# Upsampling matmuls on eight array tiles of 32x64 instead of two of 64x128, with the orders of TensorE, ScalarE and VectorE rewritten

## The chip, the cores and the metric

The kernel runs on one NeuronCore of one Trainium2 chip. The metric is the device time of one execution in microseconds, the median of several runs. The core has TensorE (PE, matmuls; its weight loads are listed as PEld), VectorE (DVE), ScalarE (ACT), GpSimd (POOL) and SyncE (SP, which here issues DMAs). Each runs its own instruction stream; they meet at semaphores only.

## What is computed

x is f32 of shape (8, 512, 128, 128). Layer 0 downsamples it with a 3x3 stride-2 convolution (256 channels, 64x64), clusters the channels, derives a gate per channel, and adds the gated and bilinearly doubled map to x. Layer 1 adds a bias, upsamples rows and columns by 2 with a 12-tap filter, applies leaky ReLU with a gain of sqrt 2, and downsamples by 2 with the 12-tap filter:

```python
def _L0(sx, w_down, w_conv, w_up):
    x = conv(sx, w_down, stride=2)             # (8, 256, 64, 64)
    ...                                        # clusters, mixture fit, gate
    pre_up = gate[:, :, None, None] * x + x
    up = jnp.repeat(pre_up, 2, axis=1) * w_up[None, :, None, None]
    return _bilinear_up_x2(up) + sx

def _L1(input, bias, up_filter, down_filter):
    out = input + bias[None, :, None, None]
    out = _sep_upfirdn(out, up_filter * 2, 2, 1, UP_PAD)     # 128x128 -> 256x256
    out = leaky_relu(out, 0.2) * sqrt(2)
    return _sep_upfirdn(out, down_filter, 1, 2, DOWN_PAD)    # 256x256 -> 128x128
```

## The kernel before

The program has five stages: `convolution`, `clusters`, `cluster_means`, `mixture` and, from about 1665 us on, `resample`. The change lies in `resample` alone.

`resample` handles the 4096 images (128x128) four at a time: a pair u is two units e of two images i, and there are PAIRS = 1024 of them. Each engine has a function `slot(u, r, m)` that issues its work of slot u; `schedule` (L863) unrolls the first and last slots and loops over the others, STEP = 4 slots to a turn, with the slot number r*4+m in registers. `cnt` gives a semaphore's target for a slot; where it depends on r, a register instruction computes it. `has(u, lag)` says whether a stage that runs `lag` slots behind has work in slot u, `after(u, n)` whether a wait is needed yet.

A pair passes these stages, in different slots:

- SP: `load_low` (L892, every second slot, two buffers), `load_img` (L904), `store` (L914).
- Every second slot (a group of two pairs): TensorE doubles the rows of the small map (L1044, `b1_acc`, in bank 6), ACT copies it (L1100, `low_v`), POOL doubles the columns (L956 to L962, `lift`). POOL adds the bias to `img` (L947).
- DVE: `x_sum` = lift*coef + img, four instructions (L1135), for pair u+1 in slot u.
- TensorE, first upsampling of pair u: `x_sum` is the stationary operand, the banded filter matrix `up_t` the moving one. The band lets the contraction over 128 rows be cut in two halves of 64; `upper` (L980) uses 133 columns of `up_t`, `lower` (L985) the other 133, on the upper and lower 64 rows of the array. Two row tiles may not write one bank at a time, so the first half of the work gives image i=0 to `upper` and i=1 to `lower`, and the second half the other way round, with the waits `u1_half`/`u2_half` on TensorE's own semaphores between. Results: `u1_acc` (banks 0, 1).
- DVE: copies both banks to `up1` (L1144).
- TensorE, second upsampling of pair u-1: the same from `up1` into `u2_acc` (banks 2 to 5).
- ACT: `slope` (L1091), a scaled copy `slope_t` of each of the four banks. DVE: `leaky` = max(GAIN*bank, slope_t) (L1152), four instructions.
- TensorE: `first_down` of pair u-2 from `leaky` into banks 6 and 7, 32 matmuls; ACT copies them (L1117, `dn1`). Then d2 of pair u-3 from `dn1` into bank 0, 16 matmuls; ACT copies it (L1108, `res`), and SP stores it. Both use L991, tiles of 128x64, 67 columns.

Order in a slot now: TensorE does first and second upsampling (first half), the group's L1044 product, their second halves, d2, `first_down`. DVE does x_sum, copies, leaky. ACT does low_v, two slopes, res, two slopes, dn1. An f32 matmul appears in the trace as two LDWEIGHTS and two MATMUL records.

Of the kernel before, what the change touches and what calls it, by code (L numbers as in the profile page):

```python
# [13 lines left out]
P = 128  # L14
# [26 lines left out]
UP_REACH = 2 * HALF + 5  # L41
# [46 lines left out]
def build(nc, x, w_down, w_conv, w_up, bias, up_filter, down_filter, consts, out):  # L88
    at = constants()[1]
    ctx = ExitStack()  # L90
    with ctx:
# [713 lines left out]
        def resample():  # L805
            with ExitStack() as own:
# [8 lines left out]
                low = [sb(f"low{i}", [HO, LOWS, WO]) for i in range(2)]  # L815
# [12 lines left out]
                low_loaded = [sem(f"low_loaded{i}") for i in range(2)]  # L828
# [7 lines left out]
                u1_half = sem("u1_half")  # L836
                u1_mm = sem("u1_mm")
                u1_out = sem("u1_out")
                u2_half = sem("u2_half")
                u2_mm = sem("u2_mm")  # L840
# [12 lines left out]
                d2_acc = bank[0]  # L853
                b1_acc = bank[6][:, 0:LOWS * WO]
# [6 lines left out]
                STEP = 4  # L861
                LOOP0, LOOP1 = STEP, PAIRS - STEP

                def schedule(eng, slot):

                    for u in range(FIRST, LOOP0):
                        slot(u, 0, u)
                    with eng.Fori(LOOP0 // STEP, LOOP1 // STEP) as r:
                        for m in range(STEP):
# [12 lines left out]
                def cnt(u, r, m, k, per=1, of=1):  # L882
# [3 lines left out]
                    return r * (STEP // of * per) + (m + k) // of * per  # L886
# [4 lines left out]
                def _(sp):  # L891
                    def load_low(u, r, m):  # L892

                        p = (m // 2) % 2
                        g = cnt(u, r, m, 4, per=2)
                        done = cnt(u, r, m, 2, of=2)
                        if u is None:
                            g, done = sp.snap(g), sp.snap(done)
                        if after(u, 0):
                            sp.wait_ge(b1_mm, done)  # L900
                        sp.dma_start(low[p][:], lows[:, bass.ds(g, LOWS), :] if u is None else lows[:, g:g + LOWS, :]).then_inc(low_loaded[p], 16)
# [20 lines left out]
                    def slot(u, r, m):  # L922
                        if m % 2 == 0 and has(u, -4):
                            load_low(u, r, m)
                        if has(u, -2):
                            load_img(u, r, m)
# [47 lines left out]
                def _(pe):  # L974

                    pe.wait_ge(ready, 2 + 2 * FT)

                    def upper(acc, src, first):

                        return pe.matmul(acc[:, 0:UP_REACH], src, up_t[0:HALF, 0:UP_REACH],  # L980
                                         start=first, stop=False, skip_group_check=True)

                    def lower(acc, src, first):

                        return pe.matmul(acc[:, UH - UP_REACH:UH], src, up_t[HALF:P, UH - UP_REACH:UH],  # L985
                                         start=first, stop=False, skip_group_check=True)
# [9 lines left out]
                    def first_up(e, i, p, half, first):  # L996
                        tile = (upper, lower)[half]
                        return tile(u1_acc[i][:, e * UH:(e + 1) * UH], x_sum[p][HALF * half:HALF * (half + 1), e, i, :], first)

                    def second_up(e, i, p, half, k, first):  # L1000
                        tile = (upper, lower)[half]
                        return tile(u2_acc[e][i][:, k * UW:(k + 1) * UW],
                                    up1[p][HALF * half:HALF * (half + 1), i, e, k * P:(k + 1) * P], first)
# [10 lines left out]
                    def slot(u, r, m):  # L1014
                        group = m % 2 == 0 and has(u, -2)
                        p = m % 2
                        if has(u, 0):
                            pe.wait_ge(x_summed, cnt(u, r, m, 1))
                            if after(u, 1):
# [166 lines left out]
```

## Time and profile before

| | us |
|---|---|
| median of 3 runs | 7928.65 (7927.54 to 7929.11) |
| profiled execution | 7925.67 |
| its span, first to last instruction | 7923.9 |
| busy: PE, DVE, ACT, POOL | 7411.7, 6318.9, 4073.0, 2543.3 |
| mean granted TensorE clock over the span | 0.969 |

The page gives busy times over the whole span, while 6.3 of its 7.9 ms are one stage, `resample`. So the page says which groups there are, the stretches say how busy each engine is in that stage, and the timeline of one slot shows who waits for whom. Records of PE overlap one another: a group's busy time is not the count times the mean. The start of a record is measured, its end modelled.

### The profile page before, as it was taken

Reading aid. Unit: us, or ns where it says so; the run is one execution under the profiler, and the core shown is the slowest. Engines: PE = TensorE matmul, PEld = TensorE weight load, DVE = VectorE, ACT = ScalarE, POOL = GpSimd, SP = SyncE. Lnnn points to the kernel's source line nnn. Section 1 sums busy time; section 2 is a strip of 40 time slices with the busy share of each in tenths; the row PEclk is TensorE's granted clock in tenths of the full one; section 3 lists DMA queues with packets and bytes.
Section 4 is the critical chain, followed back from the end, with each engine's and each line's share of the span. In section 5 each row is a group of like instructions: output and inputs, shape, how many; then the busy total and the mean of one; then the engine's idle time right before and its main releaser. Section 6 shows DMA issues by size and latency. Waiting matters only on the chain.

```text
span 7923.9 us, 374577 instructions
## 1 busy us (share of the span) xinstructions
PE 7411.7 (94%) x151493; PEld 6562.6 (83%) x151493; DVE 6318.9 (80%) x12643; ACT 4073.0 (51%) x8046; POOL 2543.3 (32%) x3076
## 2 busy tenths in 40 slices
PE   7999966069999999999999999999999999999999
PEld 3444441059999999999999999999999999999999
DVE  8999942878888888888888888888888888888887
ACT  0000002346666666666666666666666666666666
POOL 0000000024444444444444444444444444444443
PEclk9999978579999999999999999999999999999999
DMA  7777714013333333333333333333333333333333
GB/s 307 313 306 316 310 58 180 0 55 91 92 90 92 90 93 90 93 90 92 91 92 90 92 91 92 91 91 92 91 92 91 92 90 93 90 92 91 93 90 87
DMA packets 1253328, 925.41 MB, mean 117 GB/s; under 512 B 175312, under 2 KB 1224912, under 8 KB 1234384
## 3 DMA queue, kind: packets, MB, share of 16 engines
q1 hardware_dynamic: 1243920, 890.10, 34.7%
q10 hardware_dynamic: 9344, 34.61, 1.6%
q8 instruction: 22, 0.36, 0.0%
q14 instruction: 42, 0.34, 0.0%
HBM read 621.50 MB, written 303.04 MB: 117 GB/s over the span
## 4 chain that ended last, share of the span: by engine, by line
PE 79%; DVE 0%; POOL 0%; DMA 0%; ACT 0%; issue 0%; POOLq 0%; DVEq 0%
PE bank L991 38%; PE bank L980 30%; PE bank L985 9%; PE bank L1044 2%; DVE x_sum L1135 0%; DMA img<-in_x 0%; DMA low<-conv_dram 0%; ACT slope_t L1091 0%; DVE leaky L1152 0%; POOL low_f L959 0%; POOL img L947 0%; ACT dn L1117 0%; POOL low_d L956 0%; POOL lift L962 0%; ACT low_v L1100 0%
## 5 line engine op out<-in xcount | busy, mean ns | idle before, releaser
L1152 DVE SCALAR_TENSOR_TENSOR leaky<-bank,slope_t 128x512 f32<-128x512 f32 x4096 | 2637.2, 685 | 575.6 <-ACT slope_t L1091 511.2
L1091 ACT ACTIVATE slope_t<-bank 128x512 f32<-128x512 f32 x4096 | 2219.8, 597 | 1697.8 <-PE bank L985 1697.8
L980 PE MATMUL bank<-up_t,up 64*128 64x133 f32 x16384 | 2186.2, 273 | 1.4 <-DVE leaky L1152 1.2
L985 PE MATMUL bank<-up_t,up 64*128 64x133 f32 x16384 | 2186.3, 273 | 0.0
L991 PE MATMUL bank<-down_t,leaky 128*64 128x67 f32 x65536 | 2086.2, 222 | 0.0
L980 PEld LDWEIGHTS bank<-up_t,up 64*128 64x128 f32 x16384 | 2009.0, 187 | 2.4 <-DVE leaky L1152 1.0
L985 PEld LDWEIGHTS bank<-up_t,up 64*128 64x128 f32 x16384 | 2006.3, 187 | 0.0
L991 PEld LDWEIGHTS bank<-down_t,leaky 128*64 128x64 f32 x65536 | 1999.0, 137 | 0.1
L1144 DVE COPY up<-bank 128x512 f32<-128x512 f32 x2048 | 1318.7, 685 | 626.6 <-PE bank L985 626.6
L956 POOL TENSOR_TENSOR low_d<-low_v 128x252 f32<-128x252 f32 x512 | 310.9, 607 | 4023.6 <-ACT low_v L1100 4023.6
L985 PE MATMUL bank<-up_t,x_sum 64*128 64x133 f32 x8192 | 1521.0, 299 | 0.0
L947 POOL TENSOR_TENSOR img<-img,bias_all 128x512 f32<-128x512 f32 x1024 | 1064.4, 1040 | 1288.0 <-DMA img<-in_x 1288.0
L980 PE MATMUL bank<-up_t,x_sum 64*128 64x133 f32 x8192 | 1363.6, 286 | 8.5 <-DVE x_sum L1135 6.5
L980 PEld LDWEIGHTS bank<-up_t,x_sum 64*128 64x128 f32 x8192 | 1112.9, 187 | 99.1 <-DVE x_sum L1135 7.3
L991 PE MATMUL bank<-down_t,dn 128*64 128x67 f32 x32768 | 1182.4, 225 | 2.1 <-ACT dn L1117 1.5
L1135 DVE SCALAR_TENSOR_TENSOR x_sum<-lift,coef,img 128x128 f32<-128x128 f32 x4096 | 1160.6, 344 | 11.4 <-POOL img L947 8.9
L991 PEld LDWEIGHTS bank<-down_t,dn 128*64 128x64 f32 x32768 | 1039.0, 137 | 144.5 <-DVE up L1144 45.0
L1117 ACT ACTIVATE dn<-bank 128x512 f32<-128x512 f32 x2048 | 1136.2, 626 | 0.7 <-PE bank L991 0.7
L985 PEld LDWEIGHTS bank<-up_t,x_sum 64*128 64x128 f32 x8192 | 1106.7, 186 | 0.0
L252 PE MATMUL bank<-rows_in,diag 128*128 128x448 f32 (+1 forms) x2304 | 930.9, 561 | 93.4 <-DMA rows_in<-in_x 89.0
L252 PEld LDWEIGHTS bank<-rows_in,diag 128*128 128x128 f32 x2304 | 431.9, 190 | 591.7 <-issue 525.1
L231 DVE SCALAR_TENSOR_TENSOR conv<-rows_in,tap_w,conv 128x576 f32<-128x576 f32 (+3 forms) x1088 | 880.7, 809 | 45.5 <-issue 7.2
(154 smaller groups left out, 3468.3 us busy)
## 6 DMA issues: line engine op xcount, KB each, us to landing
img<-in_x SPq DMA_DIRECT2D x1024, 256.0 KB, 2.8
out<-res SPq DMA_DIRECT2D x1024, 256.0 KB, 2.2
rows_in<-in_x SPq DMA_DIRECT2D x48, 4224.0 KB, 13.9
rows_in<-in_x SPq DMA_DIRECT2D x16, 4096.0 KB, 13.9
conv_dram<-conv ACTq DMA_DIRECT2D x64, 512.0 KB, 4.1
xb<-conv_dram SPq DMA_DIRECT2D x8, 4096.0 KB, 13.3
low<-conv_dram SPq DMA_DIRECT2D x512, 64.0 KB, 2.3
xx<-conv_dram SPq DMA_DIRECT2D x2, 2048.0 KB, 9.9
```

The costliest lines, as they stand in the source:

```text
L231: ins = v.scalar_tensor_tensor(out=dst, in0=src, scalar=w, in1=dst, op0=ALU.mult, op1=ALU.add)
L252: mm = pe.matmul(acc[:, :, (1 if kw == 0 else 0):], diag[:, cb * TAPS + (i * 3 + kh) * 3 + kw, :], conv_in(n, i, kh, kw, V_ROWS, QR), star ...
L947: nc.gpsimd.tensor_tensor(pix, pix, bg[:, :, None].to_broadcast([P, 4, W]), ALU.add).then_inc(biased, 1)
L956: nc.gpsimd.tensor_tensor(low_d[:], low_v[:, :, 1:WO], low_v[:, :, 0:WO - 1], ALU.subtract).then_inc(lift_step, 1)
L980: return pe.matmul(acc[:, 0:UP_REACH], src, up_t[0:HALF, 0:UP_REACH], start=first, stop=False, skip_group_check=True)
L985: return pe.matmul(acc[:, UH - UP_REACH:UH], src, up_t[HALF:P, UH - UP_REACH:UH], start=first, stop=False, skip_group_check=True)
L991: return pe.matmul(acc[:, a:b], src, down_t[:, j, a:b], start=first, stop=False, skip_group_check=True)
L1091: nc.scalar.activation(slope_t[e][i][:], u2_acc[e][i][:], ACT.Copy, scale=SLOPE * GAIN).then_inc(slope_out, 1)
L1117: nc.scalar.activation(dn1[p][:, e].rearrange("p j i h -> p (j i h)"), d1_acc[e][:], ACT.Copy).then_inc(d1_out, 1)
L1135: ins = v.scalar_tensor_tensor(out=x_sum[n % 2][:, e, i, :], in0=lift[n // 2][:, 2 * (n % 2) + e, :], scalar=cf, in1=img[n % 2][:, e, i, : ...
L1144: v.tensor_copy(up1[m % 2][:, i].rearrange("p e h -> p (e h)"), u1_acc[i][:]).then_inc(u1_out, 1)
L1152: v.scalar_tensor_tensor(out=leaky[1 - m % 2][:, e, i].rearrange("p k w -> p (k w)"), in0=u2_acc[e][i][:], scalar=GAIN, in1=slope_t[e][i][ ...
```

## The change

Upsampling: the array is used as four row tiles of 32 by two column tiles of 64. Each contraction of 128 rows is cut in four (`UP_REACH` now holds four column ranges, 69, 74, 74 and 69 wide), each stationary operand in two halves of 64 columns (`rise`). The work of a slot is six items, one for each of the banks 0 to 5, with two halves each: 12 steps. In step t the row tile rt handles step (t - 3*rt) mod 12, so the four row tiles always write different banks; eight matmuls per step, 96 per slot. Each step's last matmul raises `up_step`, and from step 2 on TensorE waits until step t-2 has finished. The semaphores `u1_half`, `u1_mm`, `u2_half`, `u2_mm` go.

Other engines: ACT copies bank 0 to `up1` after its slopes (`u1_out0`), DVE copies bank 1 alone (`u1_out1`). DVE's slot is now copy, leaky, x_sum; ACT's is two slopes, low_v, two slopes, copy, res, dn1. TensorE's is upsampling, the group's product (now two tiles of 128x64, into bank 7), `first_down` of e=0, d2 (now into bank 1), `first_down` of e=1. `low` has one buffer of 128 rows, the lower half set to zero once. SP loads the images ahead of `low`. TensorE's loop holds two slots (PE_STEP), the others' still four.

```diff
+T = 32
+NT = P // T
+UP_REACH = [(max(0, 2 * T * r - 5), min(UH, 2 * T * (r + 1) + 5)) for r in range(NT)]
...
-                low = [sb(f"low{i}", [HO, LOWS, WO]) for i in range(2)]
+                low = sb("low", [P, LOWS, WO])
...
+                ITEMS = ((1, 0), (2, 0, 0), (2, 1, 1), (2, 0, 1), (2, 1, 0), (1, 1))
+                STEPS = 2 * len(ITEMS)
...
+                    def rise(acc, src, rt, first):
+                        a, b = UP_REACH[rt]
+                        for c in range(2):
+                            mm = pe.matmul(acc[cols(c), a:b], src[:, cols(c)], up_t[T * rt:T * (rt + 1), a:b],
+                                           start=first, stop=False, skip_group_check=True)
+                        return mm
...
+                        for t in range(STEPS if has(u, 0) or has(u, 1) else 0):
+                            if t >= 2:
+                                pe.wait_ge(up_step, cnt(u, r, m, 0, per=STEPS, step=PE_STEP) + (t - 1))
+                            for rt in range(NT):
+                                at = (t - 3 * rt) % STEPS
+                                item, half = ITEMS[at // 2], at % 2
+                                rows = slice(T * rt, T * (rt + 1))
+                                if item[0] == 1 and has(u, 0):
+                                    i = item[1]
+                                    if not used & {(1, 0), (1, 1)}:
+                                        pe.wait_ge(x_summed, cnt(u, r, m, 1, step=PE_STEP))
...
+                                if item[0] == 2 and has(u, 1):
+                                    e, i = item[1:]
...
+                                    mm = rise(u2_acc[e][i][:, half * UW:(half + 1) * UW], up1[1 - p][rows, i, e, half * P:(half + 1) * P],
+                                              rt, item not in used)
+                                    used.add(item)
+                            mm.then_inc(up_step, 1)
...
                 @block.vector
                 def _(v):
+                    v.memset(low[HO:P], 0.0).then_inc(padded, 1)
                     def slot(u, r, m):
+                        if has(u, 0):
+                            v.wait_ge(up_step, cnt(u, r, m, 1, per=STEPS))
+                            v.tensor_copy(up1[m % 2][:, 1].rearrange("p e h -> p (e h)"), u1_acc[1][:]).then_inc(u1_out1, 1)
+                        if has(u, 1):
...
+                            for e in range(2):
+                                for i in range(2):
+                                    v.wait_ge(slope_out, cnt(u, r, m, -1, per=4) + (2 * e + i + 1))
...
                         if has(u, -1):
                             n = (m + 1) % STEP
                             v.wait_ge(lifted, cnt(u, r, m, 1 + 2, of=2))
                             v.wait_ge(biased, cnt(u, r, m, 2))
-                            if after(u, 1):
-                                v.wait_ge(u1_mm, cnt(u, r, m, 0))
...
-                        if has(u, 0):
-                            v.wait_ge(u1_mm, cnt(u, r, m, 1))
...
-                            for i in range(2):
-                                v.tensor_copy(up1[m % 2][:, i].rearrange("p e h -> p (e h)"), u1_acc[i][:]).then_inc(u1_out, 1)
```

TensorE, inside the loop, the start of the upsampling before, in a slot with a group's product (128x133: 128 stationary columns, 133 moving). `[waits s]` names the semaphore that an instruction waits for:

```order
L1020 REGISTER_ALU [waits x_summed]
L1023 REGISTER_ALU [waits u1_out]
L980 MATMUL bank0<-up_t,x_sum0 128x133 [waits res_ready]
L985 MATMUL bank1<-up_t,x_sum0 128x133
L980 MATMUL bank0<-up_t,x_sum0 128x133
L985 MATMUL bank1<-up_t,x_sum0 128x133
L1033 REGISTER_ALU [waits u1_out]
L980 MATMUL bank2<-up_t,up1_1 128x133 [waits leaky_out]
L985 MATMUL bank3<-up_t,up1_1 128x133
L980 MATMUL bank2<-up_t,up1_1 128x133
L985 MATMUL bank3<-up_t,up1_1 128x133
L1033 REGISTER_ALU
```

And the same slot's product and the second half behind it:

```order
L1040 REGISTER_ALU
L1043 REGISTER_ALU [waits low_loaded0]
L1044 MATMUL bank6<-low0,cst 128x256 [waits d1_out]
L980 MATMUL bank1<-up_t,x_sum0 128x133 [waits u1_half]
L985 MATMUL bank0<-up_t,x_sum0 128x133
L980 MATMUL bank1<-up_t,x_sum0 128x133
L985 MATMUL bank0<-up_t,x_sum0 128x133
L980 MATMUL bank3<-up_t,up1_1 128x133 [waits u2_half]
L985 MATMUL bank2<-up_t,up1_1 128x133
```

TensorE now, step 0 in the loop's second slot (64x69: 64 stationary columns, 69 moving):

```order
L1027 REGISTER_ALU
L999 MATMUL bank0<-up_t,x_sum1 64x69 [waits u1_out0,x_summed]
L999 MATMUL bank0<-up_t,x_sum1 64x69
L1046 REGISTER_ALU [waits u1_out0]
L999 MATMUL bank4<-up_t,up1_0 64x74 [waits leaky_out]
L999 MATMUL bank4<-up_t,up1_0 64x74
L1046 REGISTER_ALU [waits u1_out1]
L999 MATMUL bank3<-up_t,up1_0 64x74 [waits leaky_out]
L999 MATMUL bank3<-up_t,up1_0 64x74
L1046 REGISTER_ALU [waits u1_out0]
L999 MATMUL bank2<-up_t,up1_0 64x69 [waits leaky_out]
L999 MATMUL bank2<-up_t,up1_0 64x69
```

And step 2 with the start of step 3:

```order
L1019 REGISTER_ALU
L999 MATMUL bank2<-up_t,up1_0 64x69 [waits up_step]
L999 MATMUL bank2<-up_t,up1_0 64x69
L999 MATMUL bank1<-up_t,x_sum1 64x74 x2
L999 MATMUL bank4<-up_t,up1_0 64x74 x2
L999 MATMUL bank5<-up_t,up1_0 64x69 x2
L1019 REGISTER_ALU
L999 MATMUL bank2<-up_t,up1_0 64x69 [waits up_step]
```

Where four matmuls or more followed one register instruction, two now do in step 0, and every step from 2 on begins with one and with a wait for `up_step`. The first matmul waits for `x_summed`, as it did before through L1020.

DVE before, the loop's second slot:

```order
L1126 REGISTER_ALU
L1127 REGISTER_ALU [waits lifted]
L1135 ISA [waits u1_mm,biased]
L1135 SCALAR_TENSOR_TENSOR x_sum0<-lift1,coef,img0 128x128
L1135 ISA
L1135 SCALAR_TENSOR_TENSOR x_sum0<-lift1,coef,img0 128x128
L1135 ISA
L1135 SCALAR_TENSOR_TENSOR x_sum0<-lift1,coef,img0 128x128
L1135 ISA
L1135 SCALAR_TENSOR_TENSOR x_sum0<-lift1,coef,img0 128x128
L1144 COPY up1_1<-bank0 128x512 [waits u2_mm,u1_mm]
L1144 COPY up1_1<-bank1 128x512
```

DVE now, the same slot:

```order
L1138 COPY up1_1<-bank1 128x512 [waits up_step]
L1142 REGISTER_ALU
L1145 REGISTER_ALU [waits d1_mm]
L1146 SCALAR_TENSOR_TENSOR leaky0<-bank2,slope_t0_0 128x512 [waits slope_out]
L1145 REGISTER_ALU
L1146 SCALAR_TENSOR_TENSOR leaky0<-bank3,slope_t0_1 128x512 [waits slope_out]
L1145 REGISTER_ALU
L1146 SCALAR_TENSOR_TENSOR leaky0<-bank4,slope_t1_0 128x512 [waits slope_out]
L1146 SCALAR_TENSOR_TENSOR leaky0<-bank5,slope_t1_1 128x512 [waits slope_out]
L1150 REGISTER_ALU
L1151 REGISTER_ALU [waits lifted]
L1156 ISA [waits biased]
```

The last three rows belong to x_sum, whose four instructions follow them. x_sum has moved from the slot's start to its end, behind the copy that waits for `up_step`; one copy is left.

## Rows read from the trace of the kernel before

**Rows 1.** The page: busy time, last chain, two groups, a DMA issue.

```profile
PE 7411.7 (94%) x151493; PEld 6562.6 (83%) x151493; DVE 6318.9 (80%) x12643; ACT 4073.0 (51%) x8046; POOL 2543.3 (32%) x3076
...
PE 79%; DVE 0%; POOL 0%; DMA 0%; ACT 0%; issue 0%; POOLq 0%; DVEq 0%
PE bank L991 38%; PE bank L980 30%; PE bank L985 9%; PE bank L1044 2%; DVE x_sum L1135 0%; DMA img<-in_x 0%; DMA low<-conv_dram 0%; ACT slope_t L1091 0%; DVE leaky L1152 0%; POOL low_f L959 0%; POOL img L947 0%; ACT dn L1117 0%; POOL low_d L956 0%; POOL lift L962 0%; ACT low_v L1100 0%
...
L980 PE MATMUL bank<-up_t,up 64*128 64x133 f32 x16384 | 2186.2, 273 | 1.4 <-DVE leaky L1152 1.2
...
L980 PE MATMUL bank<-up_t,x_sum 64*128 64x133 f32 x8192 | 1363.6, 286 | 8.5 <-DVE x_sum L1135 6.5
...
low<-conv_dram SPq DMA_DIRECT2D x512, 64.0 KB, 2.3
```

**Rows 2.** By stretch: length, engines' busy us, clock, DMA.

```profile
1240.00:1350.00 110.00, 93.03 (x219) 19.98 (x217) 3.64 (x2) 32.93 (x55) 0.00 (x0) 0.94 0.66 238
1350.00:1500.00 150.00, 4.40 (x14) 3.51 (x14) 134.17 (x515) 49.46 (x106) 0.00 (x0) 0.50 0.00 0
3000.00:7900.00 4900.00, 4900.00 (x116467) 4718.15 (x116466) 3959.34 (x8034) 3044.58 (x6022) 1992.96 (x2407) 1.00 0.32 91
```

**Rows 3.** Line L1135 from 3000 to 7000 us: count, duration, first and last start.

```profile
L1135 DVE SCALAR_TENSOR_TENSOR x_sum<-lift,coef,img x2623: 339/343/352, 2999.9 to 6996.0; 128x128 f32<-128x128 f32 x188
```

**Rows 4.** Timeline of PE in an upsampling: start us, length us, engine, line.

```profile
4000.15 0.27 PE L980 MATMUL bank<-up_t,up 64*128 64x133 f32 x1
4000.16 0.27 PE L985 MATMUL bank<-up_t,up 64*128 64x133 f32 x1
...
4002.19 0.27 PE L980 MATMUL bank<-up_t,up 64*128 64x133 f32 x1
```

**Rows 5.** Timeline of PE at the changes of shape and in downsampling.

```profile
4002.40 1.16 PE L991 MATMUL bank<-down_t,dn 128*64 128x67 f32 x32
...
4008.42 0.39 PE L980 MATMUL bank<-up_t,up 64*128 64x133 f32 x2
...
4008.79 0.34 PE L991 MATMUL bank<-down_t,dn 128*64 128x67 f32 x4
...
4009.77 2.04 PE L991 MATMUL bank<-down_t,leaky 128*64 128x67 f32 x64
4011.74 0.38 PE L980 MATMUL bank<-up_t,x_sum 64*128 64x133 f32 x1
```

**Rows 6.** Timeline of DVE over one slot and part of the next.

```profile
4003.30 2.71 DVE L1152 SCALAR_TENSOR_TENSOR leaky<-bank,slope_t 128x512 f32<-128x512 f32 x4 [0.40 <-ACT slope_t L1091]
4005.99 1.14 DVE L1135 SCALAR_TENSOR_TENSOR x_sum<-lift,coef,img 128x128 f32<-128x128 f32 x4
4008.04 1.29 DVE L1144 COPY up<-bank 128x512 f32<-128x512 f32 x2 [0.91 <-PE bank L985]
4009.57 1.29 DVE L1152 SCALAR_TENSOR_TENSOR leaky<-bank,slope_t 128x512 f32<-128x512 f32 x2 [0.24 <-ACT slope_t L1091]
```

**Rows 7.** Timeline of ACT, the same stretch.

```profile
4003.60 0.60 ACT L1108 ACTIVATE res<-bank 128x512 f32<-128x512 f32 x1
...
4008.94 1.09 ACT L1091 ACTIVATE slope_t<-bank 128x512 f32<-128x512 f32 x2 [1.00 <-PE bank L985]
```

**Rows 8.** Register steps on PE by line, 4011.0 to 4011.7: length ns, first start.

```profile
L1018 PEldq ALU_OP  x1: 32/32/32, 4011.1 to 4011.1; - x1
L1023 PEldq ALU_OP  x1: 32/32/32, 4011.3 to 4011.3; - x1
L1033 PEldq ALU_OP  x1: 32/32/32, 4011.4 to 4011.4; - x1
```

**Rows 9.** Timeline of PE round the L1044 product of a group slot.

```profile
4006.86 0.38 PE L1044 MATMUL bank<-low,cst 64*128 64x256 f32 x1
...
4007.08 0.27 PE L985 MATMUL bank<-up_t,x_sum 64*128 64x133 f32 x1
4007.29 0.27 PE L980 MATMUL bank<-up_t,x_sum 64*128 64x133 f32 x1
```

More of the change, by code:

```diff
@@ L861, in resample, with schedule @@
                 STEP = 4
+                PE_STEP = 2
                 LOOP0, LOOP1 = STEP, PAIRS - STEP
-                def schedule(eng, slot):
+                def schedule(eng, slot, step=STEP):
                     for u in range(FIRST, LOOP0):
                         slot(u, 0, u)
-                    with eng.Fori(LOOP0 // STEP, LOOP1 // STEP) as r:
-                        for m in range(STEP):
+                    with eng.Fori(LOOP0 // step, LOOP1 // step) as r:
+                        for m in range(step):
                             slot(None, r, m)
@@ L976, in _ @@
                     pe.wait_ge(ready, 2 + 2 * FT)
[L978 to L986, printed above, removed]
+                    pe.wait_ge(padded, 1)
                     def down(acc, src, j, first):
@@ L1038, in slot @@
                         if group:
-                            pe.wait_ge(low_loaded[(m // 2 + 1) % 2], cnt(u, r, m, 2 + 4, per=16, of=4))
+                            pe.wait_ge(low_loaded, cnt(u, r, m, 2 + 2, per=16, of=2, step=PE_STEP))
                             if after(u, 3):
-                                pe.wait_ge(d1_out, cnt(u, r, m, -3, per=2) + 1)
-                            pe.matmul(b1_acc, const("lin")[0:HALF], low[(m // 2 + 1) % 2][:].rearrange("p c w -> p (c w)"),
-                                      start=True, stop=True).then_inc(b1_mm, 1)
@@ new lines, in slot @@
+                            for c in range(2):
+                                mm = pe.matmul(b1_acc[cols(c)], const("lin")[:, cols(c)], low[:].rearrange("p c w -> p (c w)"),
+                                               start=True, stop=True)
+                            mm.then_inc(b1_mm, 1)
+                        if has(u, 2):
+                            pe.wait_ge(leaky_out, cnt(u, r, m, -1, per=4, step=PE_STEP))
+                            if after(u, 3):
+                                pe.wait_ge(d1_out, cnt(u, r, m, -3, per=2, step=PE_STEP) + 1)
+                            first_down(0, p)
@@ L1075, in slot @@
                         if has(u, 2):
-                            pe.wait_ge(leaky_out, cnt(u, r, m, -1, per=4))
+                            if after(u, 3):
+                                pe.wait_ge(d1_out, cnt(u, r, m, -2, per=2, step=PE_STEP))
                             if group:
-                                pe.wait_ge(b1_out, cnt(u, r, m, 4, of=2))
-                            for e in range(2):
-                                first_down(e, p)
-                    schedule(pe, slot)
+                                pe.wait_ge(b1_out, cnt(u, r, m, 4, of=2, step=PE_STEP))
+                            first_down(1, p)
+                    schedule(pe, slot, PE_STEP)
                 @block.scalar
@@ L1094, in slot @@
                         p = m % 2
+                        if has(u, 1):
+                            act.wait_ge(up_step, cnt(u, r, m, 1, per=STEPS))
+                            slope(u, r, m, 0)
                         if m % 2 == 0 and has(u, -2):
@@ L1101, in slot @@
                         if has(u, 1):
-                            act.wait_ge(u2_mm, cnt(u, r, m, 0))
-                            slope(u, r, m, 0)
+                            slope(u, r, m, 1)
+                        if has(u, 0):
+                            act.wait_ge(up_step, cnt(u, r, m, 1, per=STEPS))
+                            nc.scalar.activation(up1[p][:, 0].rearrange("p e h -> p (e h)"), u1_acc[0][:], ACT.Copy).then_inc(u1_out0, 1)
                         if has(u, 3):
```

116 lines of the change are left out of this document (43 added, 73 removed).

## The prediction

> **What bounds the kernel now.** I read the page first: TensorE (PE) is busy 94% of the span, and the chain that ended last is 79% PE, nearly all on the upsampling lines L980/L985 and the downsampling line L991 [rows 1]. That is an average, so the next view is the busy time by stretch: from 3000 to 7900 us PE is busy in every microsecond at a granted clock of 1.00, VectorE (DVE) 81% of it, ScalarE (ACT) 62% [rows 2]. One slot (one pair, four images) makes four x_sum instructions; 2623 of them in 4000 us are 655.8 slots, 6.10 us each [rows 3]. There are 1024 slots, so 0.1 us per slot is 102 us of time.
>
> What fills 6.10 us? Upsampling: MATMUL records come in pairs, one L980 and one L985 0.01 us apart, and the next pair stands 0.11 us later; from 4000.15 to 4002.19 are 18 steps of 0.113 us [rows 4]. An f32 matmul is two records, and each of the two lines has 24 records per slot (16384+8192 in 1024 slots [rows 1]): 24 steps, 2.72 us. Downsampling: 64 records in 2.04 us, less one record's own 0.22, are 31 steps of 0.059 us for a pair; the slot's 96 records need 2.8 us [rows 5]. The L1044 product adds 0.2 us per slot on average, the two changes of tile shape 0.20 (4002.19 to 4002.40) and 0.15 (last down record at 4011.59, next at 4011.74) [rows 4, 5]. Together 6.1: PE hardly waits for another engine, and DVE's work is hidden behind it.
>
> **The change, part 1: where x_sum stands.** This costs most, and it is not in TensorE's code. Now DVE makes x_sum(u+1) first in its slot, then the copies, then leaky (DVE's rows in the order fences). In the timeline x_sum runs from 4005.99, while PE is in the same slot's upsampling [rows 6]. In the change x_sum(u+1) stands behind a copy and the four leaky instructions, and the copy waits for up_step = 12(u+1): the end of the whole upsampling of slot u. TensorE's first instruction of upsampling u+1 waits for x_summed. So upsampling(u), DVE's slot(u), upsampling(u+1) form one serial chain, and TensorE's downsampling lies beside DVE's part.
>
> Length of DVE's part, D, from the end of the last upsampling record: ACT started its slope 0.13 after it (record end 4008.42+0.39 = 4008.81, slope 4008.94), and the first leaky started at 4009.57, so 0.76 [rows 5 to 7]. The copy ends before that (0.60 to 0.69 long). DVE's instructions in a row start 0.60 apart (two copies in 1.29, one alone 0.69). The fourth leaky starts at 0.76+1.80 = 2.56 and ends at 3.25; x_sum started 0.02 ahead of leaky's end (4003.30+2.71 against 4005.99) and took 1.14, so it ends at 4.37 [rows 6]. From a DVE end to the waiting down matmul on PE was 0.06 (4008.04+0.69 to 4008.79) [rows 5, 6]. D = 4.43. In every second slot low_v stands between the slopes on ACT and makes the third slope late by some 0.06, so 0.03 on average: D = 4.46.
>
> Beside D stands PE's remaining work, 2.8+0.2+0.35 = 3.4: hidden, and PE idles about a microsecond per slot. ACT, now with one copy more, has seven and a half instructions of 0.5 to 0.6, half a low_v, some 4.7 us from the same starting point: hidden as long as a slot is longer than 5.
>
> **Part 2: the upsampling itself, U.** Twelve steps of eight matmuls with 69 or 74 columns, two records each, replace 24 matmuls of 133 columns. If all eight tiles stream side by side a step needs 2 x 74/67 x 0.059 = 0.13 us. But from step 2 on TensorE waits for up_step, which step t-2 raises when its last matmul is done. Such a round trip can be put together from rows. After an empty array, the first four down records (two tiles, two passes) lasted 0.34 us from the first start to the last end [rows 5]; with a few columns more and one tile I keep 0.34. A waiting engine started 0.04 later (last d2 record ends 4002.40+1.16 = 4003.56, res at 4003.60) [rows 5, 7], or 0.06 as above: 0.05. Handing out eight matmuls: neighbours start 0.01 apart [rows 4], and between the register steps L1023 and L1033 four matmuls go out within the rows' 0.1 us, which L1018 to L1023, with one more register step between, need per step as well [rows 8]; I take 0.05 for eight. So 0.44 per two steps, 0.22 per step: the wait, not the columns, sets the pace. Its bounds: 0.34 (no release, no hand-out) and 0.60 (weight loads of eight tiles partly one behind another; no row shows eight).
>
> Then the start. Each per-tile wait in the loop has a target that must be computed: a register step, 0.10 us on PE's sequencer [rows 8]. Before, they were hidden because the sequencer ran ahead; behind the blocking x_summed wait they are not. Step 0 has three, so its fourth tile goes out at 0.32 and ends at 0.66; step 2 starts at 0.71. Step 1 has two in one slot and one in the next; its last tile goes out at 0.55 at most, ends at 0.89, and step 3 starts at 0.94. Step 11 starts at 0.94+4x0.44 = 2.70 and ends at 2.70+0.05+0.34 = 3.09. U = 3.1, where 2.7 stood before.
>
> **Smaller parts.** The single `low` buffer: its load waits for this slot's b1, lands 2.3 us later [rows 1] and is needed two slots on, nothing. The loop's branch falls where PE idles, nothing. The b1 product takes all 128 rows with the same columns, in the shadow of D, as is the new order of the down phases. If PE bound the slot again, these would still be level with today.
>
> **Sum.** Slot = 3.09+4.46 = 7.55 against 6.10: +1.45 us x 1024 = +1485 us. On the profiled execution's 7925.7 us that gives 9410 us; the median of the runs stands 3 us above that execution, which I leave out.
>
> **A rule against the trace.** In rows 4 two tiles start 0.01 us apart and stream side by side. The Trainium skill (TensorE: Matmul & The Clock Gate, section Measured speedup vs the span model) says that such a pack lasts one matmul plus about 4 ns per tile. By it the array's part would be 0.13 per step, and the sum would be rival 1's; the wait for up_step is what it leaves out. The same page of the Trainium skill (section The mechanism) says that matmuls start and end strictly in order. Here the trace disagrees: in a group slot's code L1044 is followed by L980 and then L985 (first order fence), and yet an L985 record starts at 4007.08, before the first L980 at 4007.29 [rows 9]. If the rule held, rival 2 would come, at its higher price.
>
> **Rivals.** (1) The completion wait is cheap, and the sequencer sets the pace: 0.10 for the register step and 0.045 for eight matmuls. Steps 0 and 1 take 0.56, ten more 1.45, the last end 0.34: U = 2.35, slot 6.81, 8650 us. For it: register steps are in the rows. Against: a release has cost 0.04 or more behind the 0.34. (2) Eight tiles don't run side by side. If weight loads went two at a time at today's 0.059 for a pair, 192 loads take 5.7 us: slot near 10.1, 12000 us; strictly in order, with one matmul per 0.067, 6.4 us, 13100 us. Against: rows 9, and that pairs overlap today both by rows and by columns. (3) The clock falls to 1.2 GHz since PE idles a microsecond per slot. Then the down phases double to 5.6 and U is near 3.8; with switches and b1 a slot is 10.2, 12100 us. Against: with PE busy 93 of 110 us the granted clock was 0.94, and 0.50 only with 4 of 150 us [rows 2]; the new slot has PE busy some 6.5 of 7.55. (4) Not slower: register steps and waits cost nothing, so that U = 12x0.128+0.05+0.17 = 1.76, and leaky doesn't wait for the slopes (D = 4.31). Slot 6.07, 7895 us. It decides from U = 1.64 at D = 4.46; the register steps of steps 0 and 1 are a third of that, so both terms must be wrong.
>
> **How the numbers follow.** Forecast 0.74: with 0.34 to 0.60 for two steps and 0.1 either way on D a slot is 7.1 to 8.3, 8950 to 10200 us. Rival 1 0.10, rival 2 0.08, rival 3 0.05, rival 4 0.03. The range takes in the forecast and rival 1 with a little room: 8500 to 10200, 0.84. Slower by over 0.2% (about what a measurement of this kernel can tell from no change) are all but rival 4, 0.97; faster 0.02, same 0.01.
>
> **What would show it.** In every slot an idle stretch of about 1 us on PE ahead of the upsampling, released by x_sum; up records in twelve bursts, two per 0.44 us, a phase of 3.1 us; DVE idle only during that phase; more than half of the chain on DVE. Bursts 0.15 apart mean rival 1; records spread evenly over a step, rival 2. All of it is wrong if the next pair's x_sum is found during the upsampling.

## The result and the profile after

The changed kernel takes 10880.6 us (median of four runs, 10879.8 to 10888.9); the kernel before, on the same chip, 7928.1 us (7926.5 to 7929.1). The ratio is 1.373, with an interval of 1.370 to 1.375: slower by 2952 us, where the prediction had 1485 us more. The profiled execution's span is 10886.9 us.

The page of the changed kernel first: engines' busy time, the last chain by engine and by line, then four groups (count, busy us, mean ns, idle before them and its releaser). They answer to [rows 1].

```profile
PE 8663.6 (80%) x299973; PEld 7526.6 (69%) x299973; DVE 6463.4 (59%) x11620; ACT 4495.8 (41%) x9070; POOL 2567.0 (24%) x3076
...
PE 38%; DVE 32%; issue 8%; ACT 4%; DVEq 2%; ACTq 0%; POOL 0%; DMA 0%; POOLq 0%
PE bank L999 35%; DVE x_sum L1156 17%; DVE leaky L1146 13%; ACT slope_t L1097 4%; PE bank L991 3%; DVE up L1138 2%; DVEq L1156 2%; DVEq L1151 0%; DVEq L1145 0%; ACTq L1096 0%; DVEq L878 0%; DVEq L1137 0%; DMA low<-conv_dram 0%; PE bank L1058 0%; POOL lift L971 0%
...
L999 PE MATMUL bank<-up_t,x_sum 32*64 32x69 f32 (+1 forms) x65536 | 3731.1, 278 | 1714.8 <-DVE x_sum L1156 1709.5
...
L1138 DVE COPY up<-bank 128x512 f32<-128x512 f32 x1024 | 708.3, 692 | 3962.6 <-PE bank L999 3962.6
...
L1146 DVE SCALAR_TENSOR_TENSOR leaky<-bank,slope_t 128x512 f32<-128x512 f32 x4096 | 2558.0, 684 | 61.6 <-ACT slope_t L1097 5.0
...
L1156 DVE SCALAR_TENSOR_TENSOR x_sum<-lift,coef,img 128x128 f32<-128x128 f32 x4096 | 2010.5, 551 | 8.0 <-POOL img L956 8.0
```

The chain that was 79% PE is now 38% PE (nearly all the upsampling line L999) and 32% DVE; L991, the downsampling, has fallen from 38% to 3%. PE idles 1709.5 us waiting for x_sum, and DVE 3962.6 us waiting for the upsampling: the two take turns. That much is the predicted serial chain, though DVE has less of the chain than the "more than half" that the prediction named as a sign. What was not predicted stands in the last row: one x_sum takes 551 ns in the mean, where [rows 3] had 343.

By stretch, as in [rows 2] (the columns after the engines are the granted clock, the DMA share and GB/s):

```profile
5000.00:8000.00 3000.00, 2441.28 (x96838) 2273.26 (x96840) 1693.38 (x3004) 1402.81 (x2838) 836.04 (x1002) 0.87 0.21 62
```

TensorE is busy 81% of the stretch, and its granted clock is 0.87, not 1.00. Line L1156 as in [rows 3]:

```profile
L1156 DVE SCALAR_TENSOR_TENSOR x_sum<-lift,coef,img x1780: 337/343/1261, 3004.0 to 6996.1; 128x128 f32<-128x128 f32 x198
```

1780 instructions are 445 slots in 4000 us: 8.99 us for a slot, where 7.55 was forecast. Most of them still take 343 ns; the longest takes 1261. The timeline of DVE over two slots shows where, and that of POOL beside it shows why (start us, length us, engine, line):

```profile
5006.30 0.69 DVE L1138 COPY up<-bank 128x512 f32<-128x512 f32 x1 [4.03 <-PE bank L999]
5007.08 2.48 DVE L1146 SCALAR_TENSOR_TENSOR leaky<-bank,slope_t 128x512 f32<-128x512 f32 x4
5009.48 1.13 DVE L1156 SCALAR_TENSOR_TENSOR x_sum<-lift,coef,img 128x128 f32<-128x128 f32 x4
5014.16 0.69 DVE L1138 COPY up<-bank 128x512 f32<-128x512 f32 x1 [3.55 <-PE bank L999]
5014.87 2.54 DVE L1146 SCALAR_TENSOR_TENSOR leaky<-bank,slope_t 128x512 f32<-128x512 f32 x4
5017.33 2.82 DVE L1156 SCALAR_TENSOR_TENSOR x_sum<-lift,coef,img 128x128 f32<-128x128 f32 x4
```

```profile
5016.39 1.12 POOL L968 TENSOR_TENSOR low_f<-low_d,cst 128x504 f32<-128x504 f32 x1
5017.58 1.11 POOL L971 TENSOR_TENSOR lift<-low_f,low_v 128x504 f32<-128x504 f32 x1
5018.64 1.09 POOL L956 TENSOR_TENSOR img<-img,bias_all 128x512 f32<-128x512 f32 x1
```

In the first slot four x_sum take 1.13 us and POOL is silent. In the second they take 2.82 us, while POOL makes lift and then adds the bias; taken one by one they last 341, 1247, 1122 and 341 ns, two of them about as long as POOL's instruction beside them. POOL has this work in every second slot only, so every second slot is longer. From the copy's start to the end of x_sum are 4.31 us in the one and 5.99 in the other.

Last, TensorE over the upsampling ahead of the first of these slots, cut to one record group of every other step, the upsampling's last group and the first group of downsampling (32x69 and 32x74 are its shapes). The last two rows are the start and the last group of the next upsampling:

```profile
5002.33 0.28 PE L999 MATMUL bank<-up_t,x_sum 32*64 32x69 f32 x2 [2.75 <-DVE x_sum L1156]
...
5003.06 0.28 PE L999 MATMUL bank<-up_t,x_sum 32*64 32x74 f32 x2
...
5003.56 0.30 PE L999 MATMUL bank<-up_t,x_sum 32*64 32x74 f32 x4
...
5004.08 0.37 PE L999 MATMUL bank<-up_t,x_sum 32*64 32x74 f32 x2
...
5004.67 0.42 PE L999 MATMUL bank<-up_t,up 32*64 32x69 f32 x6
...
5005.34 0.41 PE L999 MATMUL bank<-up_t,up 32*64 32x74 f32 x4
...
5005.85 0.35 PE L999 MATMUL bank<-up_t,up 32*64 32x74 f32 x6
5006.13 1.82 PE L991 MATMUL bank<-down_t,leaky 128*64 128x67 f32 x32
...
5010.67 0.28 PE L999 MATMUL bank<-up_t,x_sum 32*64 32x69 f32 x2 [0.85 <-DVE x_sum L1156]
...
5013.81 0.25 PE L999 MATMUL bank<-up_t,up 32*64 32x74 f32 x6
```

Step 2 starts 0.73 after step 0 (forecast 0.71). Then two steps take 0.50 to 0.52, and from 5004.08 on 0.59 to 0.67. The downsampling's first 32 records take 1.82, where each of the slot's two other groups of 32 takes 1.10. The clock has fallen to 1.2 GHz within this upsampling (granted 0.51 from 5004.1 to 5006.1), after an idle stretch of 2.75 us. The next upsampling ran at a granted clock of 1.00 and took 3.39 us from its first record to its last end (5010.67 to 5014.06); this one took 3.87.

Three things are then to be explained beside the forecast: the long x_sum, 0.50 instead of 0.44 for two steps, and the clock.

### The profile page after: what moved, and what is told of

Same layout as the page of the kernel before. It is cut to its first block, busy times and chain, and to the rows that moved or that the text cites. A ratio compares the mean times of both kernels' runs of the same rounds, so it can differ in the third digit from the quotient of the medians.

```text
span 10886.9 us, 684517 instructions
## 1 busy us (share of the span) xinstructions
PE 8663.6 (80%) x299973; PEld 7526.6 (69%) x299973; DVE 6463.4 (59%) x11620; ACT 4495.8 (41%) x9070; POOL 2567.0 (24%) x3076
## 4 chain that ended last, share of the span: by engine, by line
PE 38%; DVE 32%; issue 8%; ACT 4%; DVEq 2%; ACTq 0%; POOL 0%; DMA 0%; POOLq 0%
PE bank L999 35%; DVE x_sum L1156 17%; DVE leaky L1146 13%; ACT slope_t L1097 4%; PE bank L991 3%; DVE up L1138 2%; DVEq L1156 2%; DVEq L1151 0%; DVEq L1145 0%; ACTq L1096 0%; DVEq L878 0%; DVEq L1137 0%; DMA low<-conv_dram 0%; PE bank L1058 0%; POOL lift L971 0%
## 5 line engine op out<-in xcount | busy, mean ns | idle before, releaser
L999 PE MATMUL bank<-up_t,x_sum 32*64 32x69 f32 (+1 forms) x65536 | 3731.1, 278 | 1714.8 <-DVE x_sum L1156 1709.5
L999 PEld LDWEIGHTS bank<-up_t,x_sum 32*64 32x64 f32 x65536 | 2872.6, 152 | 1902.1 <-DVE x_sum L1156 1850.5
L999 PE MATMUL bank<-up_t,up 32*64 32x69 f32 (+1 forms) x131072 | 3689.6, 278 | 7.4 <-issue 7.4
L999 PEld LDWEIGHTS bank<-up_t,up 32*64 32x64 f32 x131072 | 3258.4, 152 | 151.9 <-issue 10.4
L1138 DVE COPY up<-bank 128x512 f32<-128x512 f32 x1024 | 708.3, 692 | 3962.6 <-PE bank L999 3962.6
L991 PE MATMUL bank<-down_t,leaky 128*64 128x67 f32 x65536 | 2655.8, 242 | 0.5 <-issue 0.3
L991 PEld LDWEIGHTS bank<-down_t,leaky 128*64 128x64 f32 x65536 | 2486.8, 156 | 150.5 <-issue 11.1
L1156 DVE SCALAR_TENSOR_TENSOR x_sum<-lift,coef,img 128x128 f32<-128x128 f32 x4096 | 2010.5, 551 | 8.0 <-POOL img L956 8.0
L991 PE MATMUL bank<-down_t,dn 128*64 128x67 f32 x32768 | 1230.7, 232 | 0.7 <-ACT dn L1126 0.7
L991 PEld LDWEIGHTS bank<-down_t,dn 128*64 128x64 f32 x32768 | 1155.5, 148 | 0.9 <-ACT dn L1126 0.9
L1119 ACT ACTIVATE res<-bank 128x512 f32<-128x512 f32 x1024 | 644.8, 630 | 184.7 <-PE bank L991 180.6
L1114 ACT ACTIVATE up<-bank 128x512 f32<-128x512 f32 x1024 | 650.2, 635 | 0.0
L968 POOL TENSOR_TENSOR low_f<-low_d,cst 128x504 f32<-128x504 f32 x512 | 570.5, 1114 | 0.0
```

The lines of the kernel that those rows point to most:

```text
L991: return pe.matmul(acc[:, a:b], src, down_t[:, j, a:b], start=first, stop=False, skip_group_check=True)
L999: mm = pe.matmul(acc[cols(c), a:b], src[:, cols(c)], up_t[T * rt:T * (rt + 1), a:b], start=first, stop=False, skip_group_check=True)
L1114: nc.scalar.activation(up1[p][:, 0].rearrange("p e h -> p (e h)"), u1_acc[0][:], ACT.Copy).then_inc(u1_out0, 1)
L1119: nc.scalar.activation(res[1 - p][:].rearrange("p i w -> p (i w)"), d2_acc[:], ACT.Copy).then_inc(res_ready, 1)
L1138: v.tensor_copy(up1[m % 2][:, 1].rearrange("p e h -> p (e h)"), u1_acc[1][:]).then_inc(u1_out1, 1)
L1156: ins = v.scalar_tensor_tensor(out=x_sum[n % 2][:, e, i, :], in0=lift[n // 2][:, 2 * (n % 2) + e, :], scalar=cf, in1=img[n % 2][:, e, i, : ...
```

## The experiments

In all of them the time of the kernel before on the same chip was 7926 to 7929 us. My theory after the result: the serial chain is the main cause, and x_sum against POOL, the round trip of 0.50 us and the clock are the rest. The rivals: the four-row tiles are slow in themselves, whatever the order; and the clock alone makes up the surplus.

**POOL's work moved away from x_sum.** In POOL's widen the wait becomes one for the x_sum of this slot, so that low_d, low_f, lift and the bias run beside the next upsampling.

```diff
-                        if after(u, 2):
-                            pool.wait_ge(x_summed, cnt(u, r, m, 0))
+                        if after(u, 0):
+                            pool.wait_ge(x_summed, cnt(u, r, m, 2))
```

> The changed kernel with one wait altered: in every second slot POOL starts its four column-doubling instructions only when this slot's x_sum (pair u+1) is made, so they run during TensorE's upsampling, when DVE is idle. Theory A (x_sum, which reads two operands from SBUF, waits for POOL's instructions in alternate slots): DVE's part falls from 6.02 to 4.31 us in those slots, x_sum's mean from 551 to about 344 ns, the slot from 8.99 to about 8.1 us, time 10880 - 870 = 10010 us (9900 to 10100). Theory B (the long slots are long because low_v stands between ACT's slopes, or because of the group's product on TensorE): nothing moves, 10880 us.

Measured: 9846.8 us, ratio 1.242 (1.240 to 1.244), 1034 us less than the changed kernel. Line L1156, and the stretch from 3000 to 8000 us:

```profile
L1156 DVE SCALAR_TENSOR_TENSOR x_sum<-lift,coef,img x2008: 337/343/349, 3004.9 to 6996.0; 128x128 f32<-128x128 f32 x183
```

```profile
3000.00:8000.00 5000.00, 4368.29 (x182045) 4052.21 (x182032) 2661.27 (x5652) 2637.45 (x5338) 1540.02 (x1883) 0.93 0.24 70
```

No x_sum is longer than 349 ns, and all slots are alike, 7.97 us. The instructions of POOL are the same ones and as many; only their time against x_sum has changed. So the collision is shown to be the cause of the long x_sum. It was worth about 0.85 us a slot (1.70 in every second one), and 1034 us is 1.01 a slot; the rest came from the clock, which rose from 0.87 to 0.93 as PE's wait for x_sum fell from 1709.5 to 1035.4 us in all. This is what the Trainium skill (SBUF — State Buffer, section Who interferes with whom) states: a VectorE instruction with two operands in SBUF and a GpSimd instruction that reads SBUF exclude one another. The trace agrees (x_sum reads lift and img), with 1247 and 1122 ns for 343. leaky, which reads one operand from a bank, keeps its pace beside low_f at 5016.39: four took 2.54 us there and 2.48 with POOL silent.

**The same, and more work for TensorE.** The 32 records of `first_down` for e=1, the last phase of TensorE's slot, are made twice; the repeats are useless and start the bank's accumulation anew, so the result stays what it was. Nothing waits for the first copy.

```diff
-                    def first_down(e, p):
+                    def first_down(e, p, inc=True):
...
-                        mm.then_inc(d1_mm, 1)
+                        if inc:
+                            mm.then_inc(d1_mm, 1)
...
+                            first_down(1, p, inc=False)
                             first_down(1, p)
```

> e1 plus useless work on TensorE: the 16 matmuls of first_down(1) are made twice in a row (same operands, same bank, same values), about 0.95 us more in the stretch where TensorE waits for x_sum. Theory A (idle stretches on TensorE lower its granted clock, and this lengthens the upsampling from 3.49 to 3.83 us): clock near 1.00 instead of 0.87, upsampling 3.5 us, slot 7.8 to 7.9 us, time 9700 to 9800 us, faster than e1 although it does more. Theory B (the clock loss has another cause, or costs nothing on the path): time that of e1 or more.

Measured: 9728.1 us, ratio 1.227 (1.225 to 1.229): with 0.95 us more work on TensorE in every slot the kernel is 119 us faster. Its stretch:

```profile
3000.00:8000.00 5000.00, 4801.97 (x205396) 4526.50 (x205392) 2701.71 (x5740) 2724.10 (x5421) 1566.76 (x1914) 1.00 0.25 71
```

The clock is 1.00 throughout. D, from the signal that ends the upsampling to the one that ends x_sum, is 4.33 us as in the run before; the upsampling went from 3.64 to 3.51 in the mean, 0.13 x 1024 = 133 us. The clock's part in the kernel with POOL's work moved is shown, and it is the small one. The rival that the clock alone makes the surplus falls: at full clock the slot is still 7.84.

**x_sum back in front, the new tiles kept.** The block of x_sum is moved to the start of DVE's slot, as it was before the change. Since the tiles of the slot before must have read the buffer, it waits for up_step.

```diff
+                        if has(u, -1):
+                            n = (m + 1) % STEP
...
+                            if after(u, 1):
+                                v.wait_ge(up_step, cnt(u, r, m, 0, per=STEPS))
...
-                        if has(u, -1):
-                            n = (m + 1) % STEP
```

> The changed kernel with x_sum back at the start of DVE's slot, ahead of the copy (with a wait for the end of the previous slot's upsampling, as before). Theory A (upsampling, DVE's slot and upsampling form a serial chain through x_sum): the chain is cut, TensorE bounds the slot with 3.5 for the upsampling and 3.45 for the rest, 6.95 to 7.2 us, granted clock 1.00, time 8800 to 9050 us; what remains above 7928 is the upsampling's own length. Theory B (the slots are long because of TensorE's waits between steps alone): upsampling stays and so does most of the time, above 10000 us.

Measured: 8327.5 us, ratio 1.050 (1.049 to 1.052). By far the largest part of the loss is gone with one block of DVE's code: 2553 of 2952 us. The collision and the half clock went with it (x_sum takes 345 ns in the mean, the clock is 1.00), so this is not the chain's price alone. The runs in a row price the parts: 1034 us for the collision with the clock that it cost, 119 for the rest of the clock, 1401 for the chain (9728.1 to 8327.5), 401 for what is left. Its last chain and its stretch:

```profile
PE 80%; issue 0%; ACT 0%; POOL 0%; DVE 0%; DMA 0%; DVEq 0%; POOLq 0%
```

```profile
3000.00:8000.00 5000.00, 4987.24 (x224021) 4646.66 (x224018) 3237.94 (x6953) 3217.72 (x6571) 1920.01 (x2320) 1.00 0.30 86
```

TensorE bounds again, at full clock. It came out faster than expected (8800 to 9050, a slot of 6.95 or more where 6.47 was measured). Little of that lies in the first steps, which stay slow:

```profile
5002.53 0.28 PE L999 MATMUL bank<-up_t,x_sum 32*64 32x69 f32 x2
...
5003.20 0.28 PE L999 MATMUL bank<-up_t,x_sum 32*64 32x74 f32 x2
```

Here step 2 starts 0.67 after step 0; in the other slots of the loop's turn it is 0.58, for 0.73 in the changed kernel. In the mean the first step is 0.11 shorter, and the signals of the twelve steps rise 0.251 apart, as they do in the changed kernel at full clock (0.250). From its first record to its last signal the upsampling takes 3.33 us of the 3.5 that were kept for it, and the rest of the slot 3.14 of 3.45: that rest, off the path in the changed kernel, had been put too high. So all of the change but the place of x_sum costs 401 us, 0.37 a slot, and the rival that the new tiles are the main cause falls. The upsampling's records span 3.25 us against 2.99 before (in slots without the product), which is 0.26 of it; no run splits the remainder.

**The order alone, on the kernel before.** Only x_sum goes to the end of DVE's slot; tiles, loop and loads are those of the kernel before.

```diff
-                        if has(u, -1):
-                            n = (m + 1) % STEP
...
+                        if has(u, -1):
+                            n = (m + 1) % STEP
```

> The kernel before with only the order on DVE changed: x_sum at the end of the slot, behind the copies and leaky. Nothing of the tiling is touched. Theory A (the order alone makes the serial chain): slot = 2.75 for the upsampling + DVE's part of 3.7 to the last leaky and 1.1 for x_sum = 7.6 us instead of 6.10, time 7928 + 1530 = 9450 us (9200 to 9800, more if the clock falls or x_sum meets POOL). Theory B (the order is harmless, the eight tiles cost it all): 7928 us.

Measured: 10982.6 us (10916.6 to 11016.4), ratio 1.387 (1.383 to 1.391). I expected 9450. The old tiles, faster with x_sum in front, are not faster here. PE's timeline over parts of one upsampling:

```profile
4017.11 0.37 PE L980 MATMUL bank<-up_t,x_sum 64*128 64x133 f32 x1 [1.94 <-DVE x_sum L1151]
...
4017.44 0.27 PE L980 MATMUL bank<-up_t,x_sum 64*128 64x133 f32 x1
...
4017.55 0.27 PE L980 MATMUL bank<-up_t,x_sum 64*128 64x133 f32 x1
...
4020.50 0.42 PE L980 MATMUL bank<-up_t,up 64*128 64x133 f32 x1
...
4020.72 0.42 PE L980 MATMUL bank<-up_t,up 64*128 64x133 f32 x1
...
4021.38 0.38 PE L980 MATMUL bank<-up_t,up 64*128 64x133 f32 x1
```

The pair's distance goes from 0.11 to 0.22 us in mid-phase: 1.2 GHz. Here the array's columns set the pace, and they take twice as long; the new tiles at half clock only went from 0.25 to 0.33 a step, which fits a pace set by a wait. Over the resample stretch the clock was 0.89 and PE busy 79%, and a slot took 9.03 us. So the order alone reaches the size of the whole loss, though by a different mix. The half clock costs more: the phase from the first to the last upsampling record took 4.14 us in the mean where it takes 3.20 in the kernel before, 0.94 a slot. And x_sum meets no POOL work here (344 ns in the mean), although it was moved here too: POOL's last instruction of a group ends at 4014.87, the x_sum behind it starts at 4015.76:

```profile
4013.83 1.04 POOL L947 TENSOR_TENSOR img<-img,bias_all 128x512 f32<-128x512 f32 x1
```

```profile
4015.76 1.13 DVE L1151 SCALAR_TENSOR_TENSOR x_sum<-lift,coef,img 128x128 f32<-128x128 f32 x4
```

The two parts of the change don't add up (3056 and 401 us apart, 2952 together).

**The round trip measured by itself.** In the kernel with x_sum in front, each step waits for the step before it instead of the one two back.

```diff
-                            if t >= 2:
+                            if t >= 1:
...
-                                pe.wait_ge(up_step, cnt(u, r, m, 0, per=STEPS, step=PE_STEP) + (t - 1))
+                                pe.wait_ge(up_step, cnt(u, r, m, 0, per=STEPS, step=PE_STEP) + t)
```

> e2 with each step waiting for the step just ahead of it, instead of for the one two ahead. Theory A (the round trip through up_step, 0.5 us, sets the pace): one round trip per step, 0.50 instead of 0.252 us, upsampling 12 x 0.25 = 3.0 us longer, slot about 9.4 us, time 11300 us (more than 11000). Theory B (columns, weight loads or register steps set the pace, the wait is mostly over when it is reached): below 9300 us.

Measured: 13335 us (two runs), ratio 1.682. PE's timeline in a stretch at full clock, the first record group of four steps in a row, and then the whole stretch:

```profile
7001.98 0.28 PE L999 MATMUL bank<-up_t,x_sum 32*64 32x74 f32 x2
...
7002.49 0.28 PE L999 MATMUL bank<-up_t,x_sum 32*64 32x74 f32 x2
...
7002.99 0.30 PE L999 MATMUL bank<-up_t,x_sum 32*64 32x74 f32 x4
...
7003.51 0.28 PE L999 MATMUL bank<-up_t,x_sum 32*64 32x74 f32 x2
```

```profile
3000.00:8000.00 5000.00, 4444.48 (x127445) 3505.79 (x127432) 1885.66 (x3956) 1894.32 (x3737) 1088.86 (x1318) 0.75 0.17 49
```

One step takes 0.503 us when one round trip lies in it, and two steps take 0.503 when one lies in two. So the wait for a step's completion sets the pace, whatever is streamed in its shadow: the predicted mechanism, with 0.503 in place of 0.44. The total is above the 11300 expected because the clock stood at half for about half of the time. A slot took 11.38 us for the 9.4 expected: the last steps went at 0.56 to 0.66, and from the last signal of an upsampling to the first of the next it took 5.18 where the run with x_sum in front, at full clock, took 3.71. These 1.47 us are the larger part. Why it did so with PE busy 89% of the stretch, while the kernel with POOL's work moved was busy 87% and had 0.93, no run here settles.

**A shorter round trip.** Again with x_sum in front; in a full slot a step's two continuing row tiles are issued first and raise up_step, and the wait stands before the two entering tiles.

```diff
-                            if t >= 2:
-                                pe.wait_ge(up_step, cnt(u, r, m, 0, per=STEPS, step=PE_STEP) + (t - 1))
-                            for rt in range(NT):
+                            step_rt = list(range(NT))
+                            if full:
+                                step_rt.sort(key=lambda rt: (t - 3 * rt) % 2 == 0)
+                            for n_rt, rt in enumerate(step_rt):
+                                if t >= 2 and n_rt == (2 if full else 0):
+                                    pe.wait_ge(up_step, cnt(u, r, m, 0, per=STEPS, step=PE_STEP) + (t - 1))
...
-                            mm.then_inc(up_step, 1)
+                                if full and n_rt == 1 and t < STEPS - 1:
+                                    mm.then_inc(up_step, 1)
```

> e2 with TensorE's order inside a step changed: the two row tiles that stay in their bank (second half of an item) go first and raise up_step; the wait for step t-2 stands behind them, ahead of the two row tiles that enter a new bank. In e2 the upsampling advances by 0.252 us per step (0.50 per two). Theory A (the round trip through up_step sets the pace): a round trip now covers three steps instead of two and half of each step's matmuls go out ahead of the wait, so the pace is about 0.20 us, the slot falls by 12 x 0.05 = 0.6 from 6.47 to 5.9 us (6.1 if leaky's release of the banks becomes the bound), time 7750 to 7950 us. Theory B (eight tiles, their weight loads or the sequencer set the pace): 0.25 us per step as before and 8327 us.

Measured: 8141.8 us, ratio 1.027 (1.025 to 1.029). It is 186 us better than with x_sum in front alone, and still not at the kernel before. The middle steps take 0.20 us, but between the first two signals are 0.39 and between the last two 0.30, 0.230 in the mean. From first record to last signal the upsampling fell from 3.33 to 2.93 us, by 0.40 of the forecast 0.6. And where PE was fast enough a new wait appears, from the list of waits (us in total, times, longest):

```profile
PE bank L991 <- DVE up L1158: 196.9, 507, 0.4
```

The down phase now comes early enough to wait for the copy on DVE: in 507 slots 0.4 us each. That is 0.19 a slot, and the slot outside the upsampling did grow by 0.21, which is about what was missing to the 7950 I had expected at most. No run takes this wait away. No version that I ran beats the kernel before.

## Why the prediction was right, and where it was wrong

**Right: the serial chain, its place and its sign.** Upsampling(u), DVE's slot, upsampling(u+1) follow one another; PE waits for x_sum, DVE for the upsampling, and downsampling is off the chain. Moving that one block back gave 2553 us, 1401 of them with the clock at 1.00 and no collision on either side (9728.1 to 8327.5); moving it alone in the old kernel cost 3056. One sign failed: DVE has 32% of the chain that ended last, not more than half, and PE 38%.

**Right: the base of D.** From the last upsampling record's end to the next one's start, as the prediction counts it, 4.46 was forecast and 4.44 measured where POOL is silent. (The 4.31 to 4.33 above run from signal to signal.) The start of the upsampling was right too, 0.73 for 0.71.

**Wrong: x_sum's duration.** That x_sum "took 1.14" was read from [rows 6], where x_sum ran while POOL had nothing in hand. The step that failed is that D was summed from durations without asking what runs beside them in the new place. The first instruction of POOL's work for a group, and the last before the next x_sum, in the kernel before:

```profile
4008.02 0.61 POOL L956 TENSOR_TENSOR low_d<-low_v 128x252 f32<-128x252 f32 x1 [4.24 <-ACT low_v L1100]
...
4010.99 1.04 POOL L947 TENSOR_TENSOR img<-img,bias_all 128x512 f32<-128x512 f32 x1
```

The last ends at 4012.03, and the next x_sum starts at 4012.39. POOL's group began 0.79 us ahead of the upsampling's end there (4008.81), and 1.62 behind it in the changed kernel (5015.68 against 5014.06), since the group's product now follows the upsampling and low_v follows two slopes. With x_sum moved alone they did not meet. By these times it took two moves of the change together to make the collision (no run moves the product alone), and the prediction had priced the second at 0.03, as the delay of a slope. The collision measured 0.85 a slot in the mean, D in all 5.29, +0.83.

**Mis-sized: the round trip.** 0.44 for two steps, measured 0.503. The 0.34 from first start to last end came from four records of two tiles [rows 5]; a step's sixteen records of eight tiles took longer. In the kernel with a wait at each step, the last matmul of a step started 0.16 us after the step's first weight load, its signal rose 0.30 after that start and the next load came 0.04 later: 0.50. Hand-out and stream are longer than I had them, the release was right. From its first record to its last end the upsampling is 3.36 in the mean of the slots at full clock, for 3.09: +0.27, of which the four round trips behind step 3 are 0.25.

**Wrong: rival 3, as all or nothing.** I gave the half clock 0.05, as a state of the whole kernel at 12100 us, since "the new slot has PE busy some 6.5 of 7.55", 86%. It came for 27% of the resample stretch. At 87% busy (POOL's work moved) it was still there, at 14% of the time; it was gone at 96%. With the x_sum collision PE's idle stretch is longer than the predicted one, which drew the clock down further. It cost 0.34 a slot here (the upsampling is 3.70 in the mean of all slots): only the upsampling's share counts, since the slowed downsampling is hidden behind DVE. The trace of the kernel before had a warning that its rows did not show, two stretches with PE busy 64 and 65% of the time and a mean granted clock between the two levels (the last three columns are the clock, the DMA share and GB/s):

```profile
960.00:1080.00 120.00, 77.23 (x239) 42.44 (x238) 86.06 (x87) 11.41 (x21) 0.00 (x0) 0.82 0.45 179
1080.00:1240.00 160.00, 103.42 (x367) 67.69 (x366) 32.67 (x174) 14.35 (x20) 0.00 (x0) 0.69 0.15 59
```

**The sum.** +0.83 +0.27 +0.34 = 1.44 us a slot on top of the forecast 7.55 makes the 8.99 measured; on the time it is 1467 us. The three were not independent: a first stall brings idle time, and idle time brings the clock.

**Rivals 1, 2 and 4** fall. The pace is not the sequencer's: a step that waits each time takes twice the time. The tiles do run side by side, four row tiles in 0.25 us at full pace. And the time isn't near 7895 in any variant. Two slips in the prediction change nothing of this: rival 2's 13100 us doesn't follow from its 6.4 us, which with D give 12800, and the code behind [rows 9] stands in the second order fence, not the first.

## What to carry to other kernels

An instruction that is moved may not keep its duration: look up what each other engine will do at the new place, in the changed order of all of them, and above all whether a VectorE instruction with two SBUF operands now meets GpSimd work. A block that feeds the bounding engine's next round belongs ahead of the work that waits for that engine's present round; here that order, with the collision and the half clock that came with it, was worth over 30%, and the rest of the change, tiles included, 5%. When TensorE begins to idle, price the half clock as a share of the time, for the phases that are on the path, rather than as yes or no.

## What the runs showed of the hardware

- The collision of the two engines stretched a 343 ns instruction to 1247 and 1122 ns, about POOL's own 1.11 and 1.09 us.
- More work on TensorE made the kernel faster: 0.95 us of useless matmuls a slot, 119 us less, with the granted clock going from 0.93 to 1.00.
- A completion wait of TensorE on its own eight-tile f32 step costs 0.503 us from step to step, against an estimate of 0.13 us for its columns, worked out from [rows 5].
- Phases that are paced by waits lose less to the half clock (0.25 to 0.33 a step) than phases paced by columns (0.11 to 0.22 a pair).
- The busy share of PE does not tell the clock: 89% busy at 0.75, 87% at 0.93, 81% at 0.87.
